# A GRU recurrence in one kernel: the input's gates multiplied by pairs of steps into the recurrence's own PSUM banks, and the state's product cut into groups of 128 columns

## What is computed

```python
def _L0_cond_ref(x, emb, ...):              # x + this
    scale, shift = jnp.split(emb @ W_emb + b_emb, 2, axis=-1)
    qkv = (_rms_norm(x, g_norm) * (1.0 + scale) + shift) @ W_qkv
    # 16 heads of 32; q and k normalized per head; softmax(q k^T / sqrt(32)) v
    return o + o @ W_out
def cell(h, x):                             # x + the scan of this over 256 steps
    i_r, i_z, i_n = jnp.split(x @ W_ih + b_ih, 3, axis=-1)
    h_r, h_z, h_n = jnp.split(h @ W_hh + b_hh, 3, axis=-1)
    r = jax.nn.sigmoid(i_r + h_r)
    z = jax.nn.sigmoid(i_z + h_z)
    n = jnp.tanh(i_n + r * h_n)
    return (1.0 - z) * n + z * h            # also the step's output
```

## Time and profile before

| what | value |
|---|---|
| median of 3 runs (lowest, highest) | 1689.05 us (1689.01, 1689.66) |
| the profiled execution's span, first to last instruction | 1688.1 us |
| TensorE matmuls busy, share of the span | 98% |
| VectorE, ScalarE, GpSimd busy | 69%, 57%, 25% |
| granted TensorE clock, mean | 1.000 |
| start of the first matmul on the state (step 0) | 686.44 us |
| issue of the last output's DMAs | 1685.40 us |

### The profile page before, as it was taken

One profiled execution on the slowest core, in us unless ns is written; L12 is line 12 of the kernel. 1 busy time (PEld: TensorE's weight loads), 2 busy tenths in 40 slices (PEclk: granted clock), 3 DMA queues, 4 the chain that ended last, 5 costly groups with the idle time before them and its releaser, 6 DMA issues.

```text
span 1688.1 us, 68257 instructions
## 1 busy us (share of the span) xinstructions
PE 1661.2 (98%) x28505; PEld 1224.4 (73%) x28505; DVE 1172.4 (69%) x4108; ACT 961.5 (57%) x3521; POOL 418.9 (25%) x477
## 2 busy tenths in 40 slices
PE   9999999999999999999999999999999999999996
PEld 7787788878888786666667666667666667666664
DVE  5888888878888876466666666666666666666665
ACT  5777777777777775344444444444444444444444
POOL 3544444444444432011111111111111111111111
PEclk9999999999999999999999999999999999999999
DMA  7244433434433326534433434434334334334331
GB/s 238 51 129 115 116 89 88 99 94 98 103 93 88 89 76 152 116 75 84 86 77 75 84 75 79 82 74 82 80 71 87 78 77 85 74 77 87 70 68 26
DMA packets 302140, 151.39 MB, mean 90 GB/s; under 512 B 142892, under 2 KB 281336, under 8 KB 301832
## 3 DMA queue, kind: packets, MB, share of 16 engines
q1 hardware_dynamic: 300368, 146.39, 39.1%
q10 hardware_dynamic: 1464, 0.63, 0.1%
HBM read 84.60 MB, written 62.13 MB: 87 GB/s over the span
## 4 chain that ended last, share of the span: by engine, by line
PE 92%; DVE 3%; DMA 1%; ACT 1%; POOL 1%; issue 1%; SPq 0%; ACTq 0%; DVEq 0%; POOLq 0%
PE ps L834 38%; PE ps L806 19%; PE ps L565 14%; PE ps L644 7%; PE ps L680 5%; PE ps L625 4%; PE ps L659 4%; PE ps L667 1%; DMA wstage<-in_L_cond_W_qkv_dram 1%; POOL rq L1515 1%; PE ps L604 0%; PE ps L586 0%; DMA GI<-gscr 0%; ACT P L1317 0%; DVE nmx L942 0%
## 5 line engine op out<-in xcount | busy, mean ns | idle before, releaser
L834 PE MATMUL ps<-whh,hT 128*32 128x192 f32 x16384 | 713.0, 326 | 12.2 <-DVE hT L1187 11.8
L834 PEld LDWEIGHTS ps<-whh,hT 128*32 128x32 f32 x16384 | 496.3, 110 | 210.6 <-DVE hT L1187 81.8
L1446 ACT ACTIVATE v<-ps 128x128 f32<-128x128 f32 x512 | 139.2, 272 | 433.4 <-PE ps L834 433.4
L806 PE MATMUL ps<-wih,x1T 128*32 128x256 f32 x6144 | 376.6, 379 | 0.0
L1580 POOL TENSOR_TENSOR outG<-hG,GI 128x128 f32<-128x128 f32 x255 | 116.8, 458 | 900.0 <-DVE hG L1180 871.8
L1161 DVE SCALAR_TENSOR_TENSOR v<-v,ps 128x64 f32<-128x64 f32 x512 | 113.0, 221 | 276.2 <-ACT v L1446 276.2
L806 PEld LDWEIGHTS ps<-wih,x1T 128*32 128x32 f32 x6144 | 200.9, 110 | 104.5 <-issue 0.4
L1317 ACT ACTIVATE P<-ps,nmx 128x256 f32<-128x256 f32 x496 | 229.2, 482 | 0.9 <-DVE nmx L942 0.9
L1454 ACT ACTIVATE v<-v 128x64 f32<-128x64 f32 x512 | 131.1, 256 | 106.6 <-DVE v L1166 106.2
L1515 POOL TENSOR_TENSOR rq<-msq,mh 128x16 f32<-128x16 f32 x64 | 185.9, 2905 | 5.3
L942 DVE TENSOR_REDUCE nmx<-ps 128x4 f32<-128x1024 f32 x128 | 155.9, 1218 | 18.3 <-PE ps L625 18.2
(11 more groups left out here) (136 smaller groups left out, 1955.0 us busy)
## 6 DMA issues: line engine op xcount, KB each, us to landing
gscr<-nat SPq DMA_DIRECT2D x96, 256.0 KB, 3.0
GI<-gscr SPq DMA_DIRECT2D x124, 192.0 KB, 4.9
xres<-in_x_dram SPq DMA_DIRECT2D x32, 256.0 KB, 3.4
xscr<-x1s SPq DMA_DIRECT2D x32, 256.0 KB, 2.4
xblk<-x1s SPq DMA_DIRECT2D x128, 64.0 KB, 2.8
GI<-xscr SPq DMA_DIRECT2D x128, 64.0 KB, 2.5
x1n<-xblk SPq DMA_DIRECT2D x124, 64.0 KB, 2.4
out_dram<-outG SPq DMA_DIRECT2D x124, 64.0 KB, 2.3
```

Of the source, the lines that this page charges most:

```text
L806: last = pe.matmul(F[G % 2][q, n], x1T[:, tt % 2, j, c, :], wih[:, c, g * D + 256 * half:g * D + 256 * half + 256], start=(c == 0), stop=( ...
L834: last = pe.matmul(ps[32 * j:32 * j + 32, q, 0:192], hT[:, 32 * c:32 * c + 32], whg[:, c, :, 128 * j + 64 * q:128 * j + 64 * q + 64], star ...
L1446: s.activation(v_rz[:, q, :], ps[:, q, 64:192], ACT.Tanh, scale=0.5).then_inc(s_tr, 1)
```

## The change

- **The input's gates go where they are needed.** A pair of steps has 2 x 16 rows, which fill the 32 columns of a column tile. TensorE multiplies them with W_ih straight into the banks of that pair: `x_group`, 12 groups of 128 columns for a pair, six behind each step's product. The banks are two sets of three, for pairs in turn: half 0 (n of h, r, n of the input), half 1, z of both halves. The stores to DRAM and back, the `GI` tiles, `keep_gate`, the three spare banks and the per-step seeds are gone. ScalarE seeds a pair's three banks with the biases once in two steps (`seed`), TensorE the first two sets (`first_seed`).
- **A step's product** is 12 groups of 128 columns, in the order `HG`: r and n of half 0, r and n of half 1, z of both halves, with the last two parts of r and n of half 0 first behind the first six groups.
- **Even and odd steps** use partitions 0 to 15 and 16 to 31 of each 32. The turned state is written into `hTE` or `hTO` with zeros beside it, and read in a window shifted by 16 columns. VectorE turns this window back into `hs` once a step (L1139 of the changed kernel), so that h of the step before stands on the partitions of the new one.
- **Elementwise:** tanh of r (64 columns, per half) and of z (128 columns, once) are separate. 1 - z moved from ScalarE to VectorE, for both halves at once; z h is one instruction of 128 columns.
- **Elsewhere:** the biases come as 20 small DMAs into `Bc` and `Bt`, in SyncE's queue in iteration b = 4 together with the four loads of the first state, and GpSimd adds them after the first stage's work. The last third of W_hh is loaded earlier. The outputs are stored in two DMAs for each earlier one.

```diff
+NPR = T // 2
+XG = [(q, c) for q in range(3) for c in range(KC)]
+HG = [(0, 0), (0, 1), (1, 0), (1, 1), (2, 0), (2, 1), (0, 2), (0, 3), (2, 2), (2, 3), (1, 2), (1, 3)]
...
+            def x_group(pr, q, c):
...
+                bank = ps[:, 3 * (pr % 2) + q, :]
+                for j in range(4):
+                    p = slice(32 * j, 32 * j + 32)
+                    if q == 2:
+                        last = pe.matmul(bank[p, 0:128], x1T[:, tt % 2, r, c, :], wih[:, c, D + 128 * j:D + 128 * j + 128],
+                                         start=False, stop=False, skip_group_check=True)
+                    else:
+                        last = pe.matmul(bank[p, 64:192], x1T[:, tt % 2, r, c, :], wrn[:, c, :, 128 * j + 64 * q:128 * j + 64 * q + 64],
+                                         start=False, stop=False, skip_group_check=True)
...
+            def h_group(t, q, c):
+                h, bank = window(t), ps[:, 3 * (t // 2 % 2) + q, :]
+                for j in range(4):
...
+                        last = pe.matmul(bank[p, 0:128], h[:, c, :], whg[:, c, 0:2, 128 * j + 64 * q:128 * j + 64 * q + 64],
+                                         start=False, stop=(c == KC - 1), skip_group_check=True)
...
             emptied(pe, ("recips", NP - 1))
-            for g in range(3):
-                for k in range(GP):
-                    gate_piece(0, g, k)
+            for q, c in XG:
+                x_group(0, q, c)
             passed(("out", NB - 1, 1))
-            for k in range(FIRST):
-                gate_piece(1, k // GP, k % GP)
-            first_seed()
+            first_seed(1)
             for t in range(T):
-                for q, c in ((0, 0), (0, 1), (1, 0), (0, 2), (0, 3), (1, 1), (1, 2), (1, 3)):
+                for q, c in HG:
...
+                    h_group(t, q, c)
+                if t // 2 + 1 < NPR:
+                    for q, c in XG[6 * (t % 2):6 * (t % 2) + 6]:
+                        x_group(t // 2 + 1, q, c)
...
+                def one_less_z():
+                    v.wait_ge(s_tz, t + 1)
+                    v.tensor_scalar(v_c, v_z, -0.5, 0.5, ALU.mult, ALU.add).then_inc(s_c, 1)
+
+                def z_times_h():
+                    v.wait_ge(s_hs, t + 1)
+                    v.scalar_tensor_tensor(out=v_h, in0=v_z, scalar=1.0, in1=hs.rearrange("p (q c) k -> p q (c k)", q=2),
+                                           op0=ALU.add, op1=ALU.mult)
...
-                gates(0)
-                one_less_z(0)
+                gate_r(0)
+                gate_z()
                 tanh_n(0)
-                gates(1)
-                seed(0)
-                one_less_z(1)
+                gate_r(1)
                 tanh_n(1)
-                seed(1)
+                if t % 2 and t // 2 + 2 < NPR:
+                    seed()
...
+            def load_biases():
+                for j in range(4):
+                    p = slice(32 * j, 32 * j + 32)
+                    for k, src in enumerate((b_hh[2 * D:3 * D], b_ih[0:D], b_ih[2 * D:3 * D], b_ih[D:2 * D])):
+                        sp.dma_start(Bc[p, k, :], src[128 * j:128 * j + 128].rearrange("(o f) -> o f", o=1)
+                                     .to_broadcast([32, 128])).then_inc(s_bl, 16)
...
+                if b == 4:
+
+                    load_biases()
                 if b:
                     store_x1(b - 1, 1)
```

More of the change, by code:

```diff
@@ L689, in turn_first_x1, with first_seed @@
                 last.then_inc(s_1T, 1)
+            def first_seed(e):
+                if e == 0:
+                    pe.wait_ge(s_bias, 2)
+                for q in range(2):
+                    pe.matmul(ps[:, 3 * e + q, 0:192], ident, Bc[:, 0:3, 64 * q:64 * q + 64], start=True, stop=False,
+                              skip_group_check=True)
+                pe.matmul(ps[:, 3 * e + 2, 0:128], ident, Bc[:, 3, :], start=True, stop=False, skip_group_check=True)
+            def x_group(pr, q, c):
+                tt, r = pr // 4, pr % 4
+                if (q, c) == (0, 0):
+                    if pr >= 2:
+                        pe.wait_ge(s_sd, 2 * (pr - 1))
+                    if pr == 0:
+                        pe.wait_ge(s_1k, 1)
+                        pe.wait_ge(s_lwi, 48)
+                    elif r == 0:
+                        pe.wait_ge(s_1c, tt)
+                bank = ps[:, 3 * (pr % 2) + q, :]
+                for j in range(4):
+                    p = slice(32 * j, 32 * j + 32)
[5 more added lines that the diff above has]
+                                         start=False, stop=False, skip_group_check=True)
+                if r == 3 and (q, c) == XG[-1]:
+                    last.then_inc(s_xd, 1)
@@ new lines, in h_group @@
+            def h_group(t, q, c):
+                h, bank = window(t), ps[:, 3 * (t // 2 % 2) + q, :]
+                for j in range(4):
+                    p = slice(32 * j, 32 * j + 32)
+                    if q == 2:
+                        last = pe.matmul(bank[p, 0:128], h[:, c, :], whh[:, c, 2 * D + 128 * j:2 * D + 128 * j + 128],
+                                         start=False, stop=(c == KC - 1), skip_group_check=True)
+                    else:
+                        last = pe.matmul(bank[p, 0:128], h[:, c, :], whg[:, c, 0:2, 128 * j + 64 * q:128 * j + 64 * q + 64],
+                                         start=False, stop=(c == KC - 1), skip_group_check=True)
+                if c == KC - 1:
+                    last.then_inc(s_sum[q], 1)
@@ L822, in _ @@
                     if (q, c) == (0, 0):
                         pe.wait_ge(s_hc, 2 * t if t else 1)
[L825 to L827 removed]
+                        if t == 0:
                             pe.wait_ge(s_lwh, 192)
[L829 to L830 removed]
                     elif (q, c) == (0, 2) and t:
                         pe.wait_ge(s_hc, 2 * t + 1)
[L833 to L836 removed]
@@ L837, in _ @@
-                    if c == KC - 1:
-                        last.then_inc(s_sum[q], 1)
-                for pt, g, k, turned in pieces(t):
-                    gate_piece(pt, g, k)
+                    h_group(t, q, c)
+                if t // 2 + 1 < NPR:
+                    for q, c in XG[6 * (t % 2):6 * (t % 2) + 6]:
+                        x_group(t // 2 + 1, q, c)
         @block.vector
```

309 lines of the change are left out of this document (96 added, 213 removed).

## The result

The changed kernel takes **1756.54 us**, the median of 4 runs (1750.52 to 1760.31), against 1689.18 (4 runs, 1689.01 to 1689.66): a ratio of 1.0396, 95% interval 1.0373 to 1.042. It is slower, as forecast, but by six times the forecast 11 us and far outside the range. The runs lie 10 us apart, where those of before lie within 0.7. The profiled execution took 1753.35 with a span of 1751.5.

A forecast was written before the change was run, and what follows sets the result against it. TensorE was taken as the bound, 3.89 us a step, with the chain at 3.88. Terms: 1688.1 - 12.9 + 21.1 + 0.1 - 1.0 + 4 = 1699.4, plus 0.95 for the runs: 1700 us, range 1685 to 1712.

The forecast's parts named there:

- 36 x 0.109 = 3.93 us, a floor for the step: Recurrence: TensorE's 36 passes of 128 columns at 0.109 us each set a least step of 3.93 us.
- The chain, 3.98: Recurrence: tanh of z, then VectorE's instructions to the next product, 3.94 to 4.00 us a step, middle 3.98; +21.1 in all.
- The rule on two columns a cycle: VectorE's 1 - z: the skill's rule would give 0.14 us and a step of 3.94; the forecast kept 3.98.
- SyncE, +4: First stage, iteration 4: 24 small DMAs delay x's loads by 5.5 to 6 us, partly hidden; +4, from 0 to 5.5.
- Between the stages, -12.9: From the x1 part to step 0: fewer, narrower passes, a DMA wait gone, a second seed; step 0 12.9 us earlier.
- The biases' sum, -1.0: First stage: VectorE's sum of the biases, 1.22 us, goes; 1.0 us saved, between 0 and 1.2.
- The end, 0: End of the kernel: 8 output DMAs instead of 4 are issued in 3.5 of the 3.8 us available; no change.
- a small idle of TensorE ended by VectorE's turn in each step: Recurrence: expected timeline sign of the forecast, along with 3.98 us from product to product.
- Rival 3: Recurrence: 0.112 passes or VectorE's semaphore waits make steps 4.03 or more, 1713 to 1718 us; chance 0.15, shared with another rival.

The follow-up runs named there:

- z earlier: The changed kernel with its bias loads at the start and h's product reordered so that z of both halves comes before n of half 1: 1750.83 us.
- a quarter sent twice: The changed kernel with a quarter of x's groups (chunk 0) sending their 128 columns twice, the number of instructions unchanged: 1772.03 us.

## Why the prediction was wrong

The sign was right, for a reason that holds: even without any late instruction the chain's 4.008 a step makes the kernel slower than before (1714 us without most of x's products). The size was wrong, by one step.

- **"36 x 0.109 = 3.93 us, a floor for the step": the step that failed.** The 0.109 holds: the steps of 3.93 us with z earlier show it. But it was taken as TensorE's only limit, with "Four weight loads in each pass fit under it, since they do in these rows". The earlier trace rows are 32 matmuls between other work; they can't show what 288 instructions in 3.9 us, step after step, want from the instruction queue. That was to be counted from the diff: the same columns in passes of 128 are 64% more instructions in the recurrence (144 loads a step instead of 88). Measured: 256 instructions of TensorE come every 3.72 us in the mean, with a shorter chain too, so 288 take 4.18. Of the miss, 4.181 - 4.020 = 0.161 in 255 steps are 41 us.
- **The chain, 3.98.** The undisturbed step is 4.007. Steps 0.256 and 0.13 apart stood as they do before; z's tanh came 2.022 + 0.437 = 2.46 behind the start of the product, forecast 2.45. 1 - z came 0.38 behind it, forecast 0.31, since two waits stand ahead of it and the second is an instruction of its own; and it took 0.14 until z h started, the lower end. Without that wait the step was 3.979. The term's error is 0.03 in 255 steps, 7 us; a further 3 are the few longer steps that stay open. VectorE's part of a step, with 1 - z at L1109 (TensorE was late ahead of these rows, so the first tanh is not at its 2.022):

```profile
1048.43 0.22 ACT L1392 ACTIVATE v<-ps 128x64 f32<-128x64 f32 x1 [2.19 <-PE ps L678]
...
1048.68 0.22 DVE L1099 SCALAR_TENSOR_TENSOR v<-v,ps 128x64 f32<-128x64 f32 x1 [1.30 <-ACT v L1392]
1048.86 0.28 ACT L1396 ACTIVATE v<-ps 128x128 f32<-128x128 f32 x1 [0.21 <-PE ps L675]
...
1049.24 0.23 DVE L1109 TENSOR_SCALAR v<-v 128x128 f32<-128x128 f32 x1
...
1049.39 0.28 DVE L1113 SCALAR_TENSOR_TENSOR v<-v,hs 128x128 f32<-128x128 f32 x1
...
1049.59 0.22 DVE L1121 TENSOR_TENSOR v<-v,v 128x64 f32<-128x64 f32 x1
```

- **The rule on two columns a cycle**, "VectorE: DVE Perf Modes", section "The perf-mode tier table", in the Trainium skill: the trace agrees: 0.14 from 1 - z's start to z h's, where z h, with two inputs and as many columns, takes 0.20 to the next start and instructions of 64 columns 0.14. That I kept the other value made no difference that counts.
- **SyncE, +4**: 6.3. The place and the delay were right: the loads are issued from 221.86 to 233.13, 11.3 us for the 11 forecast, x's loads start 5.8 us later than before for the 5.5 to 6 forecast, and ScalarE waits 7.1 us for x. That a part would be absorbed was right too: TensorE is idle for 3.1 us. What the term left out is the clock. Behind the idle stretch the granted clock is 0.50 (1.2 GHz) from 247.5 to 254.3, and the same 20 matmuls take longer. TensorE's timeline and the window of the slow part, then the chain of both kernels, the changed one first:

```profile
247.29 1.84 PE L590 MATMUL ps<-ident,P 128*128 128x128 f32 x8 [2.35 <-ACT PT L1282]
249.87 0.80 PE L511 MATMUL ps<-wqh,xh 128*128 128x512 f32 x1 [0.74 <-ACT xt L1222]
```

```profile
249.87:254.30 4.43, 4.43 (x10) 3.48 (x11) 3.38 (x6) 3.53 (x11) 2.50 (x2) 0.50 0.64 130
```

```profile
249.87 5.07 PE ps L511 x12
```

```profile
246.31 0.87 PE ps L644 x8
247.19 2.82 PE ps L565 x12
```

The 20 matmuls took 3.7 us and take 6.9; with the idle time that is the 6.3. Every kernel here with the bias loads in b = 4 has such a spell of 3.4 or 6.8 us there, and those with the loads at the start have none.

- **Between the stages, -12.9**: from the start of the x1 part to step 0 it took 20.06 us and takes 6.59, so -13.5; the first tanh of step 0 comes 0.2 sooner behind the product's start, forecast 0.1 later. **The biases' sum, -1.0**: -1.4. **The end, 0**: 0.1.
- **What was to be seen**: I named "a small idle of TensorE ended by VectorE's turn in each step". A pause of the loads of over 0.15 us at the product's start is there in 198 of 255 steps, but only 99 steps take 4.00 or 4.01: 158 pauses stand at the end of a block of instructions, which no rival had. Rival 3 named a step of 4.03 and more, by passes of 0.112 or by waits on VectorE's semaphores; neither its causes nor its size (1713 to 1718 us) is what happened.

In sum, against the forecast span of 1699.4: 41 + 7 + 3 in the steps (51.4 unrounded), 2.3 for SyncE, -0.6 between the stages, -0.3 at step 0's first tanh, -0.4 for the biases, 0.1 at the end, and -0.4 that the first stage won back behind b = 5. That is the 52.1 measured.

## What to carry to other kernels

Before splitting matmuls into narrower ones, count TensorE's instructions, loads and waits with them, and divide the time by them: here 256 took 3.72 us in the mean where instructions were late, 14.5 ns each, and at 3.78 nothing was lost. The sign in a profile is an idle "issue" in the middle of a product that no semaphore explains, at equal distances in instructions, together with more packets on the instruction queue. Where it limited, a shorter chain brought nothing; fewer and wider instructions did, and extra columns were almost free. And when a transfer that many wait for comes late, look at the granted clock behind the pause as well: here it cost as much again as the pause.

## What I had not expected of the hardware

- TensorE's instruction supply is a limit with a sharp edge: 3.72 us for 256 instructions with over a hundred gaps of over 0.25 us, 3.78 with none. It stayed at 3.72 in two orders of the work, and at 3.73 with the stores of the output left out.
- A fetch begins about 2.3 us before it is needed in the changed kernel, about 3.3 with a quarter sent twice, and about 5.0 in the kernel before (medians). A late load comes 2.2 to 3.0 us behind the start of its packet, so in the old kernel there are some 2 us to spare.
- A fetch begins near the first load of the block before its own, in no trace further ahead: in the changed kernel 50 packets have begun when the 51st boundary is reached. There, with z earlier and without the stores alike, the next packet begins 1.15 us behind a late load (median), and the load at the end of that block follows 2.6 behind its packet when it is late: 3.7 together. That reading fits the 3.72 but is only argued. In the kernel with a quarter twice the next packet begins 0.44 behind a block's first load. What sets the moment wasn't tried.
- After a gap the four column tiles can stay out of phase for the rest of a step. I saw it only where TensorE was held up; the kernel with all of x's columns repeated kept its phase with the same short passes of h.
- A second semaphore wait ahead of a VectorE instruction costs 0.07 us when it is on the path.
- After 2.35 us in which TensorE ran nothing, its granted clock was at the lower level (1.2 GHz) for 6.8 us, though it stood still for only 0.74 us of them.
